# A scan over chunks and an attention core on one Trainium2 core: inner hardware loops written out

## The reference, cut to what matters

```
# layer 0, per image: xx, z = in_proj(groupnorm(x)); xx = gelu(conv3x3(xx)), 384 channels
# xs: the 4 orders k = 0..3 (rows, columns, both also reversed); delta, B, C from projections of xs
def step(h, xs_t):
    d_t, u_t, B_t, C_t = xs_t
    dA = jnp.exp(d_t[..., None] * A)                    # 384 channels x 16 states
    h = h * dA + (d_t * u_t)[..., None] * B_t[:, :, None, :]
    y = jnp.einsum('bkdn,bkn->bkd', h, C_t)
    return (h, y)
# the four y are added, normalised, gated with gelu(z), projected to 192 channels, added to x
# layer 1, per image: q, k, v = conv3x3(qkv_proj(groupnorm(x))), 4 heads of 48 channels
attn = jax.nn.softmax(jnp.einsum('bhdn,bhdm->bhnm', q, k) * temperature, axis=-1)
out = jnp.einsum('bhnm,bhdm->bhdn', attn, v)            # projected and added to x
```

## Time and profile before

| | us |
|---|---|
| median of 3 runs | 15378.18 (15376.93 to 15384.7) |
| the profiled execution's own time | 15378.3 |
| its span, first to last instruction | 15376.4 |
| mean granted clock of PE | 0.962 of full |
| the fourth image's scan, from about | 5883 to 7202 |

### The profile page before, as it was taken

The page is one execution under the profiler, slowest core; times in us unless marked ns, Lnnn a source line. Parts: engine busy times, 40 slices in busy tenths (PEclk is TensorE's granted clock), DMA queues, the critical chain, the costliest instruction groups (busy, mean ns, idle before and its releaser), DMA issues.

```text
span 15376.4 us, 245780 instructions
## 1 busy us (share of the span) xinstructions
PE 13151.0 (86%) x60888; PEld 7921.7 (52%) x60888; DVE 12874.0 (84%) x13813; ACT 11085.9 (72%) x22746; POOL 10505.7 (68%) x4158
## 2 busy tenths in 40 slices
PE   6888888888888898888988889888898888988889
PEld 4555455554555545555455554555445554455544
DVE  8999669996799867998579985899848998499984
ACT  5887578875788657886578866788667886678865
POOL 5998069980699707997079960899608995099950
PEclk9999999999999999999999999999999999999999
DMA  3333023430234203342033420334203342033420
GB/s 110 127 127 114 20 92 128 134 98 20 96 128 137 91 20 101 128 137 87 20 109 127 135 82 20 115 128 135 75 20 120 128 135 71 20 129 126 132 66 25
DMA packets 907782, 1465.69 MB, mean 95 GB/s; under 512 B 38912, under 2 KB 891904, under 8 KB 893664
## 3 DMA queue, kind: packets, MB, share of 16 engines
q1 hardware_dynamic: 906560, 1452.37, 29.6%
HBM read 1350.07 MB, written 102.17 MB: 94 GB/s over the span
## 4 chain that ended last, share of the span: by engine, by line
PE 42%; DVE 20%; issue 20%; POOL 9%; ACT 6%; DMA 2%; DVEq 1%; ACTq 1%; POOLq 0%; SPq 0%
DVE area L1018 12%; PE ps L659 9%; PE ps L843 9%; PE ps L854 8%; POOL area L1495 7%; DVE area L1036 6%; PE ps L646 3%; PE ps L637 2%; PE ps L625 2%; ACT ps L1299 2%; POOL area L1505 2%; DMA area<-bc_rows 1%; PE ps L589 1%; PE ps L734 1%; ACT area L1268 1%
## 5 line engine op out<-in xcount | busy, mean ns | idle before, releaser
L1018 DVE TENSOR_TENSOR_SCAN area<-ps,hst,area 128x384 f32<-128x384 f32 x9216 | 8593.7, 997 | 221.3 <-ACT ps L1299 191.2
L1495 POOL TENSOR_TENSOR area<-area 128x1152 f32<-128x1152 f32 x3072 | 8001.6, 2640 | 46.0 <-POOL area L1484 28.1
L1299 ACT ACTIVATE ps<-area,a_neg 128x384 f32<-128x384 f32 x9216 | 5306.9, 581 | 1579.3 <-DVE area L1018 1379.0
L659 PE MATMUL ps<-area,ident 128*128 128x384 f32 x12672 | 4674.6, 502 | 173.3 <-ACT area L1284 129.3
L659 PEld LDWEIGHTS ps<-area,ident 128*128 128x128 f32 x12672 | 2322.4, 196 | 1861.9 <-ACT area L1284 399.1
L646 PE MATMUL ps<-ident,area 128*128 128x128 f32 x17280 | 2464.9, 280 | 5.2 <-ACT area L1268 5.2
L1479 POOL TENSOR_TENSOR area<-area,ones 128x2304 f32<-128x2304 f32 x8 | 43.3, 5414 | 3506.7 <-ACT area L1224 3386.8
L1438 ACT ACTIVATE area<-ps,t_neg,area 128x768 f32<-128x768 f32 x1728 | 1617.7, 986 | 964.8 <-PE ps L843 964.8
L646 PEld LDWEIGHTS ps<-ident,area 128*128 128x128 f32 x17280 | 2234.6, 196 | 59.2 <-ACT area L1268 9.5
L1505 POOL TENSOR_TENSOR area<-area 128x1152 f32<-128x1152 f32 x768 | 2026.9, 2639 | 129.5 <-ACT hst L1244 129.0
L637 PE MATMUL ps<-ident,area 128*128 128x128 f32 x8640 | 1481.4, 281 | 496.8 <-ACT area L1268 433.7
(11 more groups left out here) (128 smaller groups left out, 9823.3 us busy)
## 6 DMA issues: line engine op xcount, KB each, us to landing
area<-bc_rows SPq DMA_DIRECT2D x1536, 768.0 KB, 6.5
xz<-x_normed SPq DMA_DIRECT2D x144, 288.0 KB, 4.7
area<-in_x SPq DMA_DIRECT2D x18, 1728.0 KB, 10.1
area<-x_padded SPq DMA_DIRECT2D x24, 1250.0 KB, 5.6
z_raw<-z_st SPq DMA_DIRECT2D x144, 192.0 KB, 4.5
area<-z_raw SPq DMA_DIRECT2D x8, 3456.0 KB, 12.9
x_padded<-x_st SPq DMA_DIRECT2D x120, 200.0 KB, 7.3
x_normed<-area SPq DMA_DIRECT2D x9, 1728.0 KB, 7.9
```

The costliest lines, as they stand in the source:

```text
L659: m = e.matmul(ps[:, 5 + j, 0:CH], ident[:], hb[:, i % NH, j], start=i == 0, stop=i == N - 1)
L1018: e.tensor_tensor_scan(rev(hb[:, i % NH, j], k), rev(ps[:, 2 + j, 0:CH], k), rev(dbu[:, i % NH, j], k), hst[:, i, j:j + 1], ALU.mult, ALU. ...
L1299: e.activation(ps[:, 2 + j, 0:CH], dlt[:, par, j], ACT.Exp, scale=a_neg[:, j, k, i:i + 1]).then_inc(da, 1)
L1495: e.tensor_tensor(dbu[:, i % NH], du[:, par], row_b[:, q % 2, i % ROWS:i % ROWS + 1].broadcast_to([128, J, CH]), ALU.mult).then_inc(dbus, 1)
```

## The change

In `walk` the loop of two passes is gone: each engine's stream holds all 24 chunks of an image one behind the other, with the chunk number a constant everywhere. The parity of buffers and the order of the chunks are as before. In the attention core ACT's loop over three turns is written out. The loop over images stays, and so do small loops over three steps elsewhere (L713, L753, L1044, L1347, L1352, L1367).

```
         def walk(e, body):
 
-            for k in range(K):
-                last, nxt = ((k - 1, NC - 1) if k else None), ((k + 1, 0) if k < K - 1 else None)
-                body(k, 0, 0, last, (k, 1))
-                with e.Fori(0, 2) as cc:
-                    c = e.snap(2 * cc)
-                    body(k, c + 1, 1, (k, c), (k, c + 2))
-                    body(k, c + 2, 0, (k, c + 1), (k, c + 3))
-                body(k, NC - 1, 1, (k, NC - 2), nxt)
+            order = [(k, c) for k in range(K) for c in range(NC)]
+            for i, (k, c) in enumerate(order):
+                body(k, c, c % 2, order[i - 1] if i else None, order[i + 1] if i + 1 < len(order) else None)
...
                     alone(e)
-                    with e.Fori(0, 3) as c:
-                        turn = e.snap(b * 6 + c + 3 * p)
+                    for c in range(3):
+                        turn = e.snap(b * 6 + (c + 3 * p))
                         base = e.snap(turn * 36)
```

## The result

The written-out kernel takes 15293.86 us (median of 5 runs, 15287.39 to 15298.41), the kernel before 15380.8 us beside it (5 runs, 15376.93 to 15384.7). The ratio is 0.9943, 95% interval 0.9933 to 0.9954: 87 us less, where 100 were forecast. The profiled execution took 15298.41 us, the slowest of its five; its span is 15296.6 us, 80 us less than before.

The account below looks back on a forecast made before the run. POOL was taken to bound the scan at 54.65 us a chunk, disturbed by ACT's jumps back. 15378.3 us less 100 us, all other terms zero, gave 15278 us; range 15240 to 15335 us.

Parts of the forecast that it names:

- The bound and the mechanism: Scan: POOL bounds at 54.65 us a chunk; ACT's 32 jumps back disturb it; removing them saves 100 us.
- count (c): Scan: excess over 54.65 us a chunk between an image's first and last L1484, mean 12.5 us, 100 us in all.
- counts (a) and (b): Scan's loss from four long stretches an image, 92 us; from POOL's L1505 waits less each image's first, 94 us.
- DVE catching up at the end of an image's scan: End of each image's scan: DVE, running behind POOL, may catch up; 0 to 24 us in all, taken as 0.
- Loops on DVE, PE, POOL and SP at zero: Scan: writing out these engines' loops costs and gains zero; bound 15 us slower or faster.
- The bound on more fetching (1030 us): Scan's second passes: 224 more instruction packets, costed at nothing; about 1030 us if each held its engine 4.6 us.
- ScalarE's three turns at zero: Attention core: PE sets this stage, so writing out ACT's turns gains 0, at most 28 us.
- Shifted code, plus or minus 37 us: Remaining small loops and image jump move; one that starts or stops missing costs up to 4.6 us an image.
- B: Rival: nothing moves, ACT is slow at the boundary for another reason than the jump; 15378 us, chance 0.06.
- C: Rival: half the gain returns through PE's waits for POOL, clock dips or new misses; 15328 us, chance 0.09.
- D: Rival: DVE was the bound, POOL's operations shorten and the whole 191.2 us returns; 15187 us, chance 0.04.
- E: Rival: slower, DVE, PE and POOL now wait for fetches in each loop's second pass; 15457 us, chance 0.03.

Follow-up runs that it names:

- shortened product: POOL's delta x u made for one channel tile of three: in the kernel before 15325.96 us, ratio 0.9966; in the written-out kernel 15186.23 us, ratio 0.9876.
- half the rows: Kernel before, with rows of B and C loaded for half their columns only, except each direction's first chunk: 15305.26 us, ratio 0.9951.
- earlier product: POOL's delta x u issued ahead of the same step's product with B: kernel before 15430.57 us, ratio 1.003; written-out kernel 15236.18 us, ratio 0.9917.
- five increments on DVE: Written-out kernel with five increments of unused semaphores added in each step of DVE's scan: 15281.76 us, ratio 0.9936.

## Why the prediction was right, and where it was off

**The bound and the mechanism** held. ACT's jump back is the whole effect (ACT alone gives all, the others give nothing), POOL's 54.65 us a chunk is the floor, and it is what stands in all stretches after, but for the first of each image and the two with POOL's longer pause. The loss was rightly not taken as the 146.8 us of ACT nor the 191.2 us of DVE: 97 us came back in the scan against the 100 of count (c); counts (a) and (b) gave 92 and 94. POOL's own starts account for 93.5 of it.

**DVE catching up at the end of an image's scan**, 0 to 24 us, taken as 0: it gave some 4 us. From POOL's last L1479 (L1484 before) to DVE's last scan an image takes 58.4 us instead of 58.9.

**Loops on DVE, PE, POOL and SP at zero**: right by test. The bound on more fetching (1030 us) was as idle as held; straight code fetched 115 packets more on queue 8 and 45 more on queue 14 (863 against 818), 160 where 224 were counted, and pays a few microseconds, below.

**ScalarE's three turns at zero**: right, by the run that changed them alone and by the 109.2 us for two turns in both.

**Shifted code, plus or minus 37 us**, was the only term wide enough for the 13 us by which the median's gain falls short of 100. Its size is about what was lost, so the range held in part by luck: its reason was a loop that starts missing, and no new issue wait of that kind exists. What was missing in the sum is another step: everything outside the scan was taken to keep its time, and PE's granted clock had no term. At the start of the attention core it costs 2.5 us in six of eight images, 15 us. That is most of the 17 us lost outside the scan in the profiled execution; smaller parts of 1 to 3 us, of either sign, make up the rest.

**The range.** Its lower end does not follow from its terms: 37 us of shifted code and 24 us of DVE's end below 15278 are 15217 us, not 15245. The measured 15293.86 lies inside either way.

**The rivals.** B (nothing moves) and its 7 us by the branch's own price fall: a branch on ACT that misses costs 3 to 6 us in the mean. C needed new holes in half the size of the gain; what came back is 13 to 17 us. D fell, and the shortened product shows the kernel in which it would be true. E fell for this kernel, but its premise is sound in reverse: an engine that has its loop at hand gains nothing from being written out. With some 55 records more DVE's no longer was at hand.

## What to carry to other kernels

Look for "issue" as the releaser of a working engine's wait, and count it against the loop's branches; where another engine is named, compare the time from the branch to the next record of the sequencer. A short inner loop whose body has outgrown what the sequencer holds pays at every jump back, and the price depends on the DMA traffic of that moment. Then ask what the bounding engine loses at those holes, not what the waiting one does; an engine at 68% of the span can be the bound of a stage. And an edit judged in a kernel with such a jump may show the wrong sign (50 us slower looped, 55 us faster written out): remove the jump first.

## What the runs showed of the hardware that was not expected

The wait behind a jump back that misses has two parts: about 1.6 us from the start of the packet of code to the next instruction, and before that 1.7 to 4.6 us, in the mean of a kernel's 32 jumps, in which the packet has not started while SP's loads keep the DMA engines mostly 75 to 100% busy. The mean wait per jump was 3.3, 3.4, 4.9, 5.4 and 6.2 us with nothing changed on ACT (half the rows, shortened product, kernel before, all but ACT written out, earlier product).

The limit of a loop body that is still at hand lies, on DVE, between 323 and 376 of the trace's records, for loops at the places where these stood. The Trainium skill, page "Runtime: NRT & Kernel Launch", section "Instruction fetch mechanics", states that a taken branch to code outside the two resident blocks waits for a DMA. The runs agree: in each kernel that misses, a packet of instructions starts 1.6 to 1.8 us, in the mean, before the end of the 32 waits. It gives 512 instructions as the memory of most engines; a body of 376 to 378 records missed in all of 32 jumps here, so, if a record stands for one instruction, a loop has to be well below that figure.

Straight code is not quite free either. The one stretch of 54.87 us above comes between the fifth and the sixth chunk of every image, and there is one more between the eighteenth and the nineteenth: 0.3 us twice an image, 5 us in all. POOL's pause behind delta x u is 0.53 us in them in place of 0.24:

```profile
6114.88 2.61 POOL L1479 TENSOR_TENSOR area<-area 128x1152 f32<-128x1152 f32 x1
6118.02 5.21 POOL L1490 TENSOR_TENSOR area<-area 128x1152 f32<-128x1152 f32 x2 [0.53 <-POOL area L1479]
```

The repeat of the changed kernel has the same 16 pauses, and so has the written-out kernel with five increments on DVE; the kernel with ACT alone written out, where POOL keeps its loop, has none. So they come with POOL's straight code. That they are the fetch of its next piece was not tested.
